# Attention and expert layers on one core: expert outputs stored from ScalarE with rings of three, small norm operations on GpSimd, second sequence of a pair in another order

## The chip, the core and the metric

The kernel runs on one core of a Trainium2 chip. The metric is the time of one execution in microseconds. A core has five engines that run side by side, each with its own queue of instructions taken strictly in order: TensorE (PE, matmul and transposes), VectorE (DVE), ScalarE (ACT), GpSimd (POOL) and SyncE (SP, which here only issues DMAs). They are held together by semaphores, and by nothing else: the order in each queue is written out by hand.

## The reference, cut to what matters

128 sequences of 128 tokens, 256 channels. First a layer of windowed attention over another input, then a layer of 16 experts of which each token takes two, each behind a layer norm and a gate.

```python
x = x + tanh(g_xattn) * xattn(layernorm(x), ctx, ctx, wq, wk, wv, wo_w, wo_b)
x = x + tanh(g_ffn)  * ffn(layernorm(x), w_router, w_fc, w_gate, w_proj)

# xattn: q, k with rotary tables, 16 heads of 16, softmax over |key - query| <= 64, projection
scores = einsum('bhnqd,bhnkd->bhnqk', qb, kband) * sqrt(dk)
out = einsum('bhnqk,bhnkd->bhnqd', softmax(where(valid, scores, neg)), vband)

# ffn: per sequence, the 2 best of 16 experts; the first 16 tokens of an expert's list are kept
top_k_probs, positions, indices, expert_inputs = vmap(dispatch)(x, softmax(x @ w_router))
h = silu(expert_inputs @ w_gate) * (expert_inputs @ w_fc)
y = vmap(collect)(h @ w_proj, indices, positions, top_k_probs)   # sum of 2 weighted rows
```

## The kernel before

Every product is made in float32 by splitting each operand into a rounded head and a rest (`..._hi`, `..._lo`) and adding three matmuls (`split_matmul`). So next to the matmuls there are many copies (heads, on ScalarE) and subtractions (rests, on VectorE and GpSimd).

**Attention (`attention_block`, L90 to L853).** The 128 sequences go in 64 pairs. One `step(s)` on each engine works on several pairs at once: scores, softmax and values of pair s, projections of s + 1, norm and context of s + 2, statistics of s + 3, output projection of s - 1, second norm and router of s - 2. Within a pair sequence 0 comes first, then sequence 1. For each sequence: `scores` (TensorE) fills four PSUM banks ST; `partial_max` (VectorE, L496) takes their maxima; `turn_max` transposes them; `shift_of` (VectorE, L503 and L507) makes the shift; `subtract_max` (TensorE) adds it to ST; `exp_unit` (ScalarE, L352, four of them) makes the probabilities; `values_unit` (TensorE, L705) multiplies them with the values. ST is one set of banks, so the scores of the next sequence wait for the last exponential. PO, one bank, holds the turned maxima and then the values.

The orders that matter here, of one step:

- ScalarE: out_t of (s-1, 1), `normed` (L427), `normed2` (L435), `attention_head` (L393), four exponentials of sequence 0, out_t, x2t, `key_head` (L398), `copy_values` (L387), `copy_logits_t` (L381), `query_heads` (q_head L405 and the two masked copies L410), `context_head` (L370), `query_rests` (L418), four exponentials of sequence 1, `input_head` (L364).
- VectorE, second half: `partial_max(s, 1)`, `norm_stats(s+3)` (L543 to L553), `keep_logits` (L587), `shift_of(s, 1)`, `normalise(s, 0)` (L515, L517), `residual(s-1)` (L566), `residual_stats` (L573 to L583), `input_rest` (L524).
- GpSimd: `scale_of_norm2` (L319 and L321), `scale_of_norm` (L278 and L280), `residual` (L271), `rotate` of k and q (L295, L296), `query_rest` (L312), `key_rest` (L303), `context_rest` (L284).

A layer norm is spread over three engines: VectorE makes mean and variance, then `nm` = -mean and `ve` = variance + eps (128x2 elements each); GpSimd makes `rstd` = ve^-0.5 and `off` = nm * rstd; ScalarE applies them.

**Routing (L856 to L993)** makes the table of places between the two; the change doesn't touch it.

**Experts (`expert_block`, L1030 to L1302).** 128 units, one per step; a unit is a sequence where tokens are moved, and two of the 16 experts of a group of eight sequences where products are made. `step(u)` does each stage for unit u - lag, with the lags LOAD -13, PICK -11, DISPATCH -9, GATE 0, HIDDEN 2, OUTPUT 3, FETCH 12, COLLECT 14. So in step u VectorE collects unit u - 14, whose rows GpSimd fetched in step u - 12. Buffers are rings: `eo`, `first`, `second`, `y_sb` have two slots, `x_in_sb` and `xr` four. GpSimd and SyncE have the steps written out flat (`run_flat`); ScalarE, VectorE and TensorE loop over 16 of them (`run`). The places that matter:

- SyncE, per step: wait for `out_done` of this step's collect, store `out` (L1118); load `xn2` (L1124); wait for `eo_copied`, store `eo_d`, 256 KB (L1129); load `xr`, 128 KB (L1134).
- GpSimd, per step: wait for the group's `eo_out` and for `out_done` of the unit two before (the ring of `first` and `second`), two indirect gathers (L1150), then `x_lo` (L1159).
- VectorE, per step: `h_lo` (L1205), `pick` (L1210), `y_part` (L1220), `gated` (L1228), `hid` (L1232), `y_sb` (L1237), `s_lo` (L1243).
- ScalarE, per step: `eo` (L1171, waits for the store of two units before), `h_hi` (L1176), `x_hi` (L1182), `th` (L1187), `s_hi` (L1193).

## Time and profile before

| | |
|---|---|
| median of 3 runs | 1889.34 us (1888.83 to 1892.42) |
| the profiled execution | 1888.86 us, span of its instructions 1887.1 us |
| mean granted TensorE clock | 0.957 |
| attention, routing, experts | 0 to about 1240, 1240 to 1340, 1340 to 1887 us |
| busy in attention (480 to 864 us) | PE 89%, DVE 82%, ACT 73%, POOL 51% |
| busy in experts (1429.5 to 1805 us) | PE 83%, DVE 83%, POOL 72%, ACT 52%, DMA 75% |

Times are microseconds from the start of the span. "PE" is TensorE's matmuls, "PEld" its weight loads, SPq the issues on SyncE's queue. A busy engine isn't necessarily the one that sets the pace: in both stages no engine is over 90%, so the waits between engines have to be read.

### The profile page before, as it was taken

The numbers are of one execution on the slowest core, as the hardware profiler recorded it, in microseconds if no ns is written. First come the engines' busy times: TensorE is split into PE (matmuls) and PEld (weight loads), VectorE is DVE, ScalarE is ACT, GpSimd is POOL, SyncE is SP. The second block draws the span as 40 slices with busy tenths as digits, with TensorE's granted clock in tenths as the row PEclk, the third lists the DMA queues.
The fourth block names the chain that finished last, engine by engine and source line by source line (L and its number), as shares of the span: only waits on it lengthen the run. The fifth ranks groups of instructions, "written<-read, shape, count | busy, mean of one in ns | idle before, by whom it ended". The sixth has DMA issues, their size and how long they took to land. (4 is left out here: it accounts for less than half of the span.)

```text
span 1887.1 us, 51499 instructions
## 1 busy us (share of the span) xinstructions
PE 1528.9 (81%) x16844; PEld 1200.2 (64%) x16844; DVE 1483.6 (79%) x3249; ACT 1165.1 (62%) x2321; POOL 1023.6 (54%) x1234
## 2 busy tenths in 40 slices
PE   4888888888888888888888888961597888788870
PEld 3566666666666666666666666640487777777760
DVE  3788888888888888888888888859788888888863
ACT  3777677777777776777777777742364555555530
POOL 3545555545545454555555545427346677677755
PEclk9999999999999999999999999975699999999995
DMA  2121212122121212121212122420257777777775
GB/s 87 46 84 56 83 56 76 63 71 68 65 74 57 82 56 83 56 83 56 83 56 81 58 68 71 137 89 12 62 170 224 231 240 236 229 240 236 239 212 178
DMA packets 156085, 210.12 MB, mean 111 GB/s; under 512 B 18688, under 2 KB 104832, under 8 KB 156032
## 3 DMA queue, kind: packets, MB, share of 16 engines
q1 hardware_dynamic: 143744, 175.92, 28.8%
q0 software_dynamic: 12288, 33.57, 6.4%
q8 instruction: 24, 0.39, 0.1%
q14 instruction: 29, 0.24, 0.0%
HBM read 125.54 MB, written 83.89 MB: 111 GB/s over the span
## 5 line engine op out<-in xcount | busy, mean ns | idle before, releaser
L496 DVE TRANSPOSE_TENSOR_REDUCE part_max<-ST 128x16 f32<-128x512 f32 x512 | 321.1, 684 | 151.0 <-PE ST L678 151.0
L705 PE MATMUL PO<-probs_t,v_aug 128*32 128x128 f32 x4096 | 206.1, 285 | 79.1 <-ACT probs_t L352 59.2
L352 ACT ACTIVATE probs_t<-ST 128x512 f32<-128x512 f32 x512 | 264.3, 602 | 8.6 <-PE ST L693 8.6
L705 PEld LDWEIGHTS PO<-probs_t,v_aug 128*32 128x32 f32 x4096 | 84.9, 108 | 194.8 <-ACT probs_t L352 188.2
L312 POOL TENSOR_TENSOR q_rest<-q_rot,q_head 128x512 f32<-128x512 f32 x64 | 82.5, 1289 | 217.3 <-ACT q_head L405 217.3
L295 POOL TENSOR_TENSOR k_rot<-k_cos,k_sin 128x256 f32<-128x256 f32 x64 | 47.2, 737 | 259.0 <-DVE k_sin L534 259.0
L1171 ACT ACTIVATE eo<-EO 128x512 f32<-128x512 f32 x128 | 76.6, 598 | 177.6 <-DMA eo_d<-eo 177.1
L1150 POOL DMA_INDIRECT first<-eo_d,collect_row x128 | 123.3, 963 | 107.1 <-DVE y_sb L1237 84.3
L1253 PE MATMUL GU<-we_hi,s_hi 128*128 128x256 f32 x512 | 156.2, 305 | 0.1
L1150 POOL DMA_INDIRECT second<-eo_d,collect_row x128 | 125.4, 980 | 42.8 <-issue 36.3
L1254 PE MATMUL GU<-we_hi,s_lo 128*128 128x256 f32 x512 | 145.5, 284 | 0.0
L1255 PE MATMUL GU<-we_lo,s_hi 128*128 128x256 f32 x512 | 144.9, 283 | 0.0
L1159 POOL TENSOR_TENSOR x_lo<-scaled,x_hi 128x256 fp32r<-128x256 f32 x128 | 109.1, 853 | 49.9 <-ACT x_hi L1182 47.6
L1253 PE MATMUL EO<-we_hi,h_hi 128*128 128x256 f32 x256 | 80.8, 316 | 54.9 <-ACT h_hi L1176 34.8
L1182 ACT ACTIVATE x_hi<-scaled 128x256 fp32r<-128x256 f32 x128 | 53.4, 417 | 113.4 <-PE DS L1298 67.7
L393 ACT ACTIVATE at_hi<-F 128x512 fp32r<-128x512 f32 x64 | 38.3, 598 | 133.1 <-PE F L723 133.1
L1297 PE MATMUL DS<-pick,x_hi 128*128 128x256 f32 x256 | 78.0, 325 | 51.4 <-DVE s_lo L1243 24.5
L1220 DVE SCALAR_TENSOR_TENSOR y_part<-first,weight,scaled 128x256 f32<-128x256 f32 x128 | 69.1, 540 | 58.2 <-DMA second<-eo_d,collect_row 54.6
L319 POOL TENSOR_TENSOR rstd<-ve,mhalf 128x2 f32<-128x2 f32 x64 | 44.9, 702 | 124.1 <-DVE ve L583 124.1
L358 ACT ACTIVATE out_t<-PO 128x512 f32<-128x512 f32 x128 | 76.7, 599 | 56.6 <-PE PO L705 53.2
L427 ACT ACTIVATE xn<-x_in_sb,off,rstd 128x256 f32<-128x256 f32 x128 | 70.0, 594 | 64.1 <-POOL off L280 64.1
L723 PE MATMUL F<-ident_sb,xn 128*128 128x128 f32 x512 | 85.7, 291 | 28.6 <-ACT xn L427 19.3
(158 smaller groups left out, 5731.0 us busy)
## 6 DMA issues: line engine op xcount, KB each, us to landing
eo_d<-eo SPq DMA_DIRECT2D x128, 256.0 KB, 2.6
x_in_sb<-x SPq DMA_DIRECT2D x64, 256.0 KB, 2.8
c_in_sb<-ctx_t SPq DMA_DIRECT2D x64, 256.0 KB, 2.8
xr_sb<-x SPq DMA_DIRECT2D x64, 256.0 KB, 4.0
x_d<-x SPq DMA_DIRECT2D x64, 256.0 KB, 4.0
xn_d<-xn SPq DMA_DIRECT2D x64, 256.0 KB, 4.2
scaled<-xn_d SPq DMA_DIRECT2D x128, 128.0 KB
scaled<-x_d SPq DMA_DIRECT2D x128, 128.0 KB
```

Of the source, the lines that this page charges most:

```text
L312: pool.tensor_tensor(q_rest[:].rearrange("p k t -> p (k t)"), q_rot[:].rearrange("p k t -> p (k t)"), q_head[:].rearrange("p k t -> p (k t ...
L352: act.activation(probs_t[:, b, i].rearrange("p j q -> p (j q)"), ST[i][:], ACT.Exp) \
L358: act.activation(out_t[:, b].rearrange("p i q -> p (i q)"), PO[:], ACT.Copy).then_inc(M["ot_copied"], 1)
L496: dve.tensor_reduce(part_max[:, i, 0], ST[i][:].rearrange("p (c l) -> p c l", l=32), AX_X, ALU.max, apply_transpose=True).then_inc(M["part ...
L705: last = pe.matmul(PO[32 * j:32 * j + 32, i * SEQ:(i + 1) * SEQ], v_aug[:, n.par, b, head], probs_t[:, b, i, j], start=True, stop=True)
L723: last = pe.transpose(F[:, (2 * k + b) * SEQ:(2 * k + b + 1) * SEQ], src[:, b, k * P:(k + 1) * P], ident[:])
L1150: pool.indirect_dma_start(out=dst[:, n.slot(2)], out_offset=None, in_=D["eo_d"][n.group].rearrange("r e c -> (r e) c"), in_offset=bass.Ind ...
L1159: pool.tensor_tensor(x_lo[:, n.slot(2)], x_in_sb[:, n.slot(4)], x_hi[:, n.slot(2)].bitcast(F32), ALU.subtract).then_inc(M["x_lo_done"], 1)
L1253: pe.matmul(out, lh, rh, start=first, stop=False)
L1254: pe.matmul(out, ll, rh, start=False, stop=False)
L1255: return pe.matmul(out, lh, rl, start=False, stop=last)
L1297: pe.matmul(out, x_hi[:, n.slot(2), k * P:(k + 1) * P], pick[:, n.slot(2)], start=True, stop=False)
```

## The change

Four things, all in the order or the place of work; what is computed stays.

1. Norms: `nm` and `ve` (and `nm2`, `ve2`) are made on GpSimd, right before `rstd`, instead of on VectorE after the aggregates. GpSimd waits for `ln_aggr` instead of `ve_done`.
2. Attention, sequence 1 of a pair. VectorE: `shift_of(s, 1)` before `keep_logits`, `residual` before `normalise`. TensorE: `logits_t` after `output_projection(.., 1)`, `subtract_max` before `untranspose`, `inputs_t` between `values_unit` 1 and 2. ScalarE: q_head and the masked copies before `copy_values`, `context_head` after the exponentials.
3. Experts: the store of `eo_d` is issued by ScalarE, behind `h_hi`. `eo`, `first`, `second`, `x_in_sb`, `xr` are rings of three. So the store is waited for three units later, and a gather waits for the collect of three units before, which is the step before its own. `y_part` is written in place in `y_sb` (its wait for the store of `out` moves up by one instruction), `gated` in place in `th`.
4. Experts: ScalarE and VectorE are written out flat too.

```diff
         def scale_of_norm(n):
+            pool.wait_ge(M["ln_aggr"], (n + 1).n)
+            wait_for(pool, M["xn_done"], n.n)
+            pool.sem_inc(M["pool_passed"], 1)
+            pool.tensor_scalar(ve[:], mv[:, :, 1], EPS, None, ALU.add).then_inc(M["ve_done"], 1)
+            pool.tensor_scalar(nm[:], mv[:, :, 0], -1.0, None, ALU.mult)
             pool.wait_ge(M["ve_done"], (n + 1).n)
-            wait_for(pool, M["xn_done"], n.n)
             pool.tensor_tensor(rstd[:], ve[:], mhalf[:], ALU.pow).then_inc(M["rstd_done"], 1)
...
             if (s + 1).real:
                 key_head(s + 1)
+                query_head(s + 1)
+                masked_heads(s + 1)
                 copy_values(s + 1)
             if (s - 2).real:
                 copy_logits_t(s - 2)
             if (s + 1).real:
-                query_heads(s + 1)
-            if (s + 2).real:
-                context_head(s + 2)
-            if (s + 1).real:
-                query_rests(s + 1)
+                masked_rests(s + 1)
             if s.real:
                 for i in range(4):
                     exp_unit(s, 1, i)
             if (s + 2).real:
+                context_head(s + 2)
                 input_head(s + 2)
...
-            dve.wait_ge(M["ln_aggr"], (n + 1).n)
-            wait_for(dve, M["off_done"], n.n)
-            dve.tensor_scalar(nm[:], mv[:, :, 0], -1.0, None, ALU.mult)
-            dve.tensor_scalar_add(ve[:], mv[:, :, 1], EPS).then_inc(M["ve_done"], 1)
...
                 norm_stats(s + 3)
+            if s.real:
+                shift_of(s, 1)
             if (s - 2).real:
                 keep_logits(s - 2)
+            if (s - 1).real:
+                residual(s - 1)
             if s.real:
-                shift_of(s, 1)
                 normalise(s, 0)
             if (s - 1).real:
-                residual(s - 1)
                 residual_stats(s - 1)
...
                 output_projection(s - 1, 0)
-            if (s - 2).real:
-                logits_t(s - 2)
             if s.real:
                 turn_max(s, 1)
             if (s - 1).real:
                 output_projection(s - 1, 1)
+            if (s - 2).real:
+                logits_t(s - 2)
             if s.real:
+                subtract_max(s, 1)
                 untranspose(s, 0)
-                subtract_max(s, 1)
+                values_unit(s, 1, 0)
+                values_unit(s, 1, 1)
             if (s + 2).real:
                 inputs_t(s + 2)
             if s.real:
-                for i in range(4):
-                    values_unit(s, 1, i)
+                values_unit(s, 1, 2)
+                values_unit(s, 1, 3)
...
-            n = unit(OUTPUT)
-            if on(OUTPUT):
-                sp.wait_ge(M["eo_copied"], n.n + 1)
-                sp.dma_start(D["eo_d"][n.group][:, n.j * 2:n.j * 2 + 2], eo[:, n.slot(2)]) \
-                    .then_inc(eo_out[n.slot(2)], 16)
             n = unit(FETCH)
             if on(FETCH):
-                wait_for(sp, M["y_part_done"], n.n - 3)
...
+                wait_for(sp, M["y_part_done"], n.n - 2)
...
-                wait_for(pool, M["out_done"], n.n - 1)
+                wait_for(pool, M["out_done"], n.n - 2)
...
                 act.wait_ge(M["eo_done"], n.n + 1)
-                wait_for(act, eo_out[n.slot(2)], (n - 2).landed(2))
-                act.activation(flat(eo[:, n.slot(2)]), EO[n.slot(2)][:], ACT.Copy).then_inc(M["eo_copied"], 1)
+                wait_for(act, eo_out[n.turn(3)], (n - 3).landed(3))
+                act.activation(flat(eo[:, n.turn(3)]), EO[n.slot(2)][:], ACT.Copy).then_inc(M["eo_copied"], 1)
...
+            n = unit(OUTPUT)
+            if on(OUTPUT):
+                act.wait_ge(M["eo_copied"], n.n + 1)
+                act.dma_start(D["eo_d"][n.group][:, n.j * 2:n.j * 2 + 2], eo[:, n.turn(3)]) \
+                    .then_inc(eo_out[n.turn(3)], 16)
...
-                dve.wait_ge(rows_in[n.slot(2)], n.landed(2, 32))
-                dve.wait_ge(x1_in[n.slot(4)], n.landed(4))
-                wait_for(dve, M["out_done"], n.n)
-                dve.scalar_tensor_tensor(out=y_part[:], in0=first[:, n.slot(2)],
+                dve.wait_ge(rows_in[n.turn(3)], n.landed(3, 32))
+                dve.wait_ge(x1_in[n.turn(3)], n.landed(3))
+                wait_for(dve, y_out[n.slot(2)], (n - 2).landed(2))
+                dve.scalar_tensor_tensor(out=y_sb[:, n.slot(2)], in0=first[:, n.turn(3)],
...
-        run(dve, step)
+        run_flat(dve, step)
```

## Rows read from the trace of the kernel before

**Rows 1.** First and last start of an instruction of each step: attention, early experts, collects, tail.

```profile
L364 ACT ACTIVATE xt_hi<-F x57: 628/628/628, 110.9 to 1182.0; 128x512 fp32r<-128x512 f32 x57
L1193 ACT ACTIVATE s_hi<-DS x10: 589/591/593, 1359.4 to 1385.6; 128x512 fp32r<-128x512 f32 x10
L1237 DVE SCALAR_TENSOR_TENSOR y_sb<-second,weight,y_part x96: 476/686/1072, 1429.7 to 1801.0; 128x256 f32<-128x256 f32 x96
L1237 DVE SCALAR_TENSOR_TENSOR y_sb<-second,weight,y_part x15: 479/485/485, 1838.4 to 1884.4; 128x256 f32<-128x256 f32 x15
```

**Rows 2.** Timeline (start, duration, what, [idle before]), sequence 1 of a pair in attention.

```profile
603.30 1.29 POOL L312 TENSOR_TENSOR q_rest<-q_rot,q_head 128x512 f32<-128x512 f32 x1 [3.44 <-ACT q_head L405]
603.42 0.33 PE L686 MATMUL PO<-ident_sb,part_max 128*128 128x128 f32 x1
603.54 1.07 DVE L552 TENSOR_SCALAR nm<-mv 128x2 f32<-128x2 f32 x1
604.70 0.28 DVE L503 TENSOR_REDUCE PO<-PO 128x32 f32<-128x128 f32 x1
605.01 0.69 DVE L507 TENSOR_TENSOR shift<-PO,own_sb 128x512 fp32r<-128x512 f32 x1
605.08 1.32 ACT L418 ACTIVATE q_lo<-q_rest,qmask_sb 128x512 fp32r<-128x512 f32 x2
606.38 2.06 ACT L352 ACTIVATE probs_t<-ST 128x512 f32<-128x512 f32 x4
608.21 0.17 DVE L582 TENSOR_SCALAR nm<-mv 128x2 f32<-128x2 f32 x1
```

**Rows 3.** Timeline, from there to the next pair's first exponentials.

```profile
605.77 1.29 POOL L284 TENSOR_TENSOR ct_lo<-c_in_sb,ct_hi 128x512 fp32r<-128x512 f32 x1
608.31 0.63 ACT L364 ACTIVATE xt_hi<-F 128x512 fp32r<-128x512 f32 x1
608.61 0.70 POOL L319 TENSOR_TENSOR rstd<-ve,mhalf 128x2 f32<-128x2 f32 x1 [1.55 <-DVE ve L583]
609.39 0.20 POOL L321 TENSOR_TENSOR off<-nm,rstd 128x2 f32<-128x2 f32 x1
610.63 1.10 ACT L427 ACTIVATE xn<-x_in_sb,off,rstd 128x256 f32<-128x256 f32 x2 [1.04 <-POOL off L280]
614.84 0.60 ACT L393 ACTIVATE at_hi<-F 128x512 fp32r<-128x512 f32 x1 [2.13 <-PE F L723]
615.41 2.07 ACT L352 ACTIVATE probs_t<-ST 128x512 f32<-128x512 f32 x4
...
627.66 0.63 ACT L364 ACTIVATE xt_hi<-F 128x512 fp32r<-128x512 f32 x1
```

**Rows 4.** The chain (start, duration, what) through two steps of the expert stage.

```profile
1636.62 0.49 DVE y_sb L1237
...
1639.15 3.59 DMA second<-eo_d,collect_row
...
1644.65 0.48 DVE y_sb L1237
```

**Rows 5.** The chain, elsewhere in the same stage: the load of xr.

```profile
1605.21 4.24 DMA scaled<-x_d
```

**Rows 6.** Groups, 1429.5 to 1805 us: count | busy us, mean ns | idle before.

```profile
L1159 POOL TENSOR_TENSOR x_lo<-scaled,x_hi 128x256 fp32r<-128x256 f32 x96 | 84.4, 879 | 2.0
L1171 ACT ACTIVATE eo<-EO 128x512 f32<-128x512 f32 x96 | 57.4, 598 | 138.0 <-DMA eo_d<-eo 137.9
```

**Rows 7.** Timeline of the expert stage, GpSimd and VectorE.

```profile
1601.24 0.42 DVE L1205 TENSOR_TENSOR h_lo<-HT,h_hi 128x256 fp32r<-128x256 f32 x1 [0.47 <-ACT h_hi L1176]
...
1604.39 0.42 DVE L1205 TENSOR_TENSOR h_lo<-HT,h_hi 128x256 fp32r<-128x256 f32 x1
...
1604.59 0.96 POOL L1150 DMA_INDIRECT first<-eo_d,collect_row  x1 [0.19 <-issue]
...
1606.83 0.75 POOL L1159 TENSOR_TENSOR x_lo<-scaled,x_hi 128x256 fp32r<-128x256 f32 x1
```

More of the change, by code:

```diff
@@ L1025, in slot, with turn @@
         return self.c % ring
+    def turn(self, ring):
+        return self.n % ring
     def landed(self, ring, each=16):
-        return (self.i * (LOOP // ring) + self.c // ring + 1) * each
+        return (self.n // ring + 1) * each
 def expert_block(nc, ctx, T, D):
@@ L1055, in expert_block @@
     th = sb("th", [P, 2, 2, HID])
-    gated = sb("gated", [P, 2, HID])
     hid = sb("hid", [P, 2, 2, HID])
@@ L1059, in expert_block @@
     h_lo = sb("h_lo", [P, 2, 2, P], F32R)
[L1060 to L1064 removed]
+    eo = sb("eo", [P, 3, 2, DIM])
+    first = sb("first", [P, 3, DIM])
+    second = sb("second", [P, 3, DIM])
     ident, iota = T["ident2"], T["iota"]
@@ L1158, in step @@
                 wait_for(pool, M["ds_done"], n.n - 1)
-                pool.tensor_tensor(x_lo[:, n.slot(2)], x_in_sb[:, n.slot(4)], x_hi[:, n.slot(2)].bitcast(F32),
+                pool.tensor_tensor(x_lo[:, n.slot(2)], x_in_sb[:, n.turn(3)], x_hi[:, n.slot(2)].bitcast(F32),
                                    ALU.subtract).then_inc(M["x_lo_done"], 1)
@@ L1235, in step @@
                 dve.wait_ge(M["y_part_done"], n.n + 1)
-                wait_for(dve, y_out[n.slot(2)], (n - 2).landed(2))
-                dve.scalar_tensor_tensor(out=y_sb[:, n.slot(2)], in0=second[:, n.slot(2)],
-                                         scalar=weight[:, 1, bass.ds(n.n, 1)], in1=y_part[:],
+                dve.scalar_tensor_tensor(out=y_sb[:, n.slot(2)], in0=second[:, n.turn(3)],
+                                         scalar=weight[:, 1, bass.ds(n.n, 1)], in1=y_sb[:, n.slot(2)],
                                          op0=ALU.mult, op1=ALU.add).then_inc(M["out_done"], 1)
```

72 lines of the change are left out of this document (35 added, 37 removed).

## The prediction

> **What bounds the kernel now.** I read the pace of each stage first. In attention a pair takes (1182.0 - 110.9) / 56 = 19.13 us [rows 1]. In the expert stage a step takes (1801.0 - 1429.7) / 95 = 3.91 us while products are made, and (1884.4 - 1838.4) / 14 = 3.29 us in the tail, where only rows are collected; the first steps, before anything is collected, took (1385.6 - 1359.4) / 9 = 2.91 us [rows 1]. So TensorE could do a step in 2.9 us, and collecting costs a microsecond more.
>
> Then what closes the circle in each stage. *Experts:* the chain of waits runs from one collect to the collect two steps later [rows 4]. `y_sb` ends at 1637.11; the first gather and the issue of the second take it to 1639.15, and the second one's landing 3.59 us more; `y_sb` of that unit ends at 1645.13. That is 8.02 us for two steps, 4.01 per step, against 3.91 measured. The circle has two steps because the ring of `first` and `second` has two slots. A second circle of the same length runs over SyncE: `y_sb`, store of `out`, load, store of `eo_d`, load of `xr`, which landed 4.24 us after its issue began [rows 5], with three issues of nearly half a microsecond ahead of it. ScalarE sat idle for 138.0 us before 96 `eo` copies, 1.44 us each, for a store of `eo_d` to land [rows 6]. *Attention:* no engine is full, the work goes through all of them in turn. Between turned maxima (ready at 603.75) and VectorE's `neg` (604.70) nearly a microsecond is lost: VectorE is held in `nm`, 1.07 us for two elements per partition, which ends with GpSimd's `q_rest` (603.30 + 1.29 = 604.59); the same instruction took 0.17 us at 608.21 with GpSimd idle [rows 2]. ScalarE is late as well: `q_lo` ends at 606.40 and the exponentials start at 606.38, though the shift was ready at 605.70.
>
> **The change, part by part.** *Sequence 1 in attention.* `nm` leaves VectorE and `shift_of` goes ahead of `keep_logits`, so `neg` waits for the turned maxima alone: 604.70 becomes about 603.7, as `logits_t` no longer stands ahead of `turn_max` either. The shift is ready 1.0 us earlier, at about 604.7. ScalarE must be free by then. It moves q_head and the masked copies into the time that it waited for the value projection, and `context_head` (0.6 us) behind the exponentials; `q_rest` starts earlier and ends before `q_lo` wants it. I get ScalarE free at about 604.5. So the exponentials start 1.0 us earlier. `inputs_t`, now between values 1 and 2, fills a gap in which TensorE waits for exponentials; `untranspose` runs beside the first one. Gain 1.0 us per pair up to the end of the exponentials, bounds 0.6 and 1.1.
>
> *What is late next.* From that end E (608.44 in [rows 2]) to the next pair's first exponential took 615.41 - 608.44 = 6.97 us [rows 3]. This pair is one of the longer: 627.66 - 608.31 = 19.35 [rows 3] against the mean of 19.13 [rows 1], so the mean is 6.75 and the shorter ones, which alternate with these, have about 6.5. The moves put a new chain here. `context_head` 0.5, then `ct_lo` on GpSimd 1.29, which used to be done long before E (605.77 to 607.06) and now stands in front of the norms. Then per norm two added operations, `rstd` 0.70, 0.08 of wait, `off` 0.20. Then `xn` and, as long, `xn2` on ScalarE, 1.0 each, and `at_hi` 0.6, ahead of the exponentials in ScalarE's order [rows 3]. The price of an added GpSimd operation on 128x2 is in no row. The nearest are `off`, 0.20 (a plain multiply of the same size), and `rstd`, 0.70 (a power) [rows 3]; VectorE's own 0.17 [rows 2] bounds it from below. I take 0.18, a plain multiply with its overlap. Sum: 0.5 + 0.1 + 1.25 + 2 x (0.36 + 0.94) + 0.1 + 2.0 + 0.6 = 7.15 us. That is 0.4 more than the mean 6.75. It was covered before by the 1.04 and 2.13 us that ScalarE idled for `off` and for the transposed attention [rows 3]; both covers are used up. So the net is 1.0 - 0.4 = 0.6 to 0.65 per pair; over some 60 pairs 39 us. By the ends of the price: at 0.17 nothing changes, at 0.70 the sum is 2.1 us longer, and a pair loses 1.5 us instead. The other readers in that stretch have room: key projection wants `ct_lo`, ready at E + 1.9, only behind the next scores and a transpose, and VectorE's `xt_lo`, which may end a little after those scores, is covered by ScalarE's chain.
>
> The rows show VectorE's `nm` held until GpSimd's instruction is over [rows 2]. [...]
>
> *Rings of three.* The gather now waits for the collect of the step before its own. The circle of 8.0 us has three steps in place of two: 2.7 per step, no longer a bound. In the tail the circle is shorter (3.29 x 2 = 6.6), so 2.2 per step, about GpSimd's own two gathers: 2.24 from first to `x_lo` [rows 7]. I take 2.35.
>
> *The store of `eo_d` on ScalarE.* SyncE loses one issue of about 0.5 us and 256 KB ahead of `xr` in its queue. The `xr` circle, 1.4 + 4.24 + 2.1 from `y_part` to the end of `y_sb` = 7.7 per two steps, becomes 0.9 + 3.0 to 4.24 + 2.1, 3.0 to 3.6 per step; without those 256 KB I place it at the lower end, under the next bound. With three slots `eo` has a step more to land, and the 1.44 us of ScalarE go. ScalarE pays the issue, about 0.5 us beside 52% of 3.91, 2.0 of work: 2.5 per step. Queued behind it are `x_hi`, `th`, `s_hi`; VectorE waits for `th`. That is under the next bound too. The price on ScalarE is in no row; between nothing and 1 us I take SyncE's 0.5. `x_in_sb` and `xr` lose a slot; SyncE then waits for `x_lo` and `y_part` of the step before, both done before the `out_done` for which it waits anyway: nothing.
>
> *What is late next in the expert stage.* GpSimd: first gather at 1604.59, `x_lo` at 1606.83 for 0.75 to 1.0 us (mean 0.88), 0.19 of issue [rows 6, 7]: 2.24 + 0.88 + 0.19 = 3.3 us. VectorE: from `h_lo` at 1601.24 to `h_lo` at 1604.39 without a wait but one: 3.15 us, with a `y_sb` of 0.55; with the median `y_sb` of 0.69 it is 3.3 [rows 1, 7]. Written flat, it also drops some register operations. Two engines at 3.3 that hold each other up: I take 3.45, bounds 3.3 and 3.75. Steps with collect and products: about 113, 113 x (3.91 - 3.45) = 51 us. Tail: 14 x (3.29 - 2.35) = 13 us. Experts 64 us.
>
> **Sum.** The profiled execution took 1888.86 us (span 1887.1 and 1.8 around it), 0.5 under the median of the runs shown. 1889 - 39 - 64 = 1786 us.
>
> **The rivals.** *Experts gain, attention doesn't.* An added GpSimd operation costs about 0.35, or ScalarE isn't free when the shift is ready: the chain behind E takes back the whole microsecond. 1889 - 64 = 1825. For it: the chain was worked out to 7.15 against 6.5 in half of the pairs, so there is little room. Against: a plain multiply was 0.20. Chance 0.22.
>
> *VectorE's collects wait for GpSimd.* [...] GpSimd, now 72% busy, would be over 90%, and if each `y_sb` took its longest, 1.07, and `y_part` as much more, a step would be 3.15 + 0.5 + 0.3 = 3.9: only the tail and attention gain, 1889 - 39 - 13 = 1837. For it: the spread of `y_sb` and `x_lo` in [rows 1, 7]. [...] Halfway, at 3.7, it is 1815. [...] Chance 0.15 for 1815 to 1840.
>
> *Better than forecast.* Attention keeps the whole microsecond (60 us) and a step falls to 3.3 (69 us): 1889 - 60 - 69 - 13 = 1747. Chance 0.12 for under 1765.
>
> *Slower.* The four added operations stand in series on GpSimd between E and the next exponentials. At x us each they cost 60 x 4 x (x - 0.18) more than in the sum, against 103 us gained: the sum turns at x = 0.18 + 103 / 240 = 0.61. At 0.70, the price of `rstd`, it is 1786 + 125 = 1911. For it: a GpSimd operation is long for its size. Against: the 0.20 of `off`. Chance 0.03.
>
> *It doesn't do what it says:* the gathers still wait for `out_done`, since GpSimd waits for `eo_out` of the whole group, which lands later. The last store of a group is issued two steps before its first gather, and a landing as long as that of [rows 5] fits in 6.9. Then a group would lose up to 1 us, 16 in all: 1802, inside the forecast.
>
> **How the numbers follow.** Forecast 1786 with a range of its own from 1765 to 1812, chance 0.48. The range for 8 in 10 takes in the attention rival and half of the lock rival, and part of the better case: 1752 to 1836. A measurement of this kernel can tell 0.2% from no change, 1885.6 to 1893.1. Faster 0.95, within 0.02, slower 0.03.
>
> **What would show it.** Attention right: `neg` follows the turned maxima at once, the exponentials start about 0.6 us behind the shift and ScalarE has no idle time between `xn` and `at_hi`; a pair takes 18.5 us. Wrong: GpSimd's added operations are over 0.3 us, or `q_lo` still ends with the start of the exponentials. Experts right: no idle time before `eo` for a store, gathers not behind `y_sb`, 3.45 us a step and 2.35 in the tail. Wrong: `y_sb` and `y_part` near a microsecond, or idle time before `y_part` for `xr`. The prediction fails most if either engine finds a new partner to wait for that I haven't costed.

## The result, and the profile after

The changed kernel took 1835.47 us (median of 4 runs, 1834.73 to 1839.67), the kernel before 1889.93 beside it: ratio 0.9717, with an interval of 0.9696 to 0.9737. The forecast was 1786. The direction was right, and the gain was about half of what the sum said. The time lies outside the range that the forecast gave itself, 1765 to 1812, and half a microsecond inside the range for 8 in 10, 1752 to 1836. The profiled execution took 1835.99 us, with a span of 1834.2.

| stretch | before | after | forecast |
|---|---|---|---|
| start to the first `y_sb` (attention, routing, first expert steps) | 1398.1 us | 1402.5 us | -39 us |
| a pair in attention | 19.13 us | 19.20 us | 18.5 us |
| collects 0 to 113 | 440.3 us | 393.1 us | -51 us |
| an expert step | 3.91 us | 3.46 us | 3.45 us |
| the 14 steps of the tail | 45.9 us | 36.0 us | -13 us |
| mean granted TensorE clock | 0.957 | 0.936 | |

An expert step is the mean from collect 0 to collect 103, here and below; up to collect 113 the mean is 3.90 before and 3.48 after.

So the experts gave 57 us where 64 were expected, and attention gave back 4 where 39 were expected. The rows that answer to [rows 1] are these: first `xt_hi`, one per pair, then `y_sb` while products are made and in the tail. `y_sb` now goes by the name `scaled`, since the rings share one tile; its input `second` tells it from `y_part`.

```profile
L372 ACT ACTIVATE xt_hi<-F x57: 617/620/622, 112.0 to 1187.2; 128x512 fp32r<-128x512 f32 x57
...
L1243 DVE SCALAR_TENSOR_TENSOR scaled<-second,weight,scaled x105: 477/701/1066, 1402.5 to 1761.4; 128x256 f32<-128x256 f32 x105
L1243 DVE SCALAR_TENSOR_TENSOR scaled<-second,weight,scaled x15: 478/485/551, 1795.6 to 1831.5; 128x256 f32<-128x256 f32 x15
```

**Attention: sequence 1 went as forecast.** The rows below (start, duration, what, idle before) answer to [rows 2]. The turned maxima are no longer held behind `nm`: the reduction is followed by the shift and, 0.67 us behind the shift's end (607.72 + 0.69 = 608.41), by the exponentials.

```profile
606.64 1.33 ACT L428 ACTIVATE q_lo<-q_rest,qmask_sb 128x512 fp32r<-128x512 f32 x2
607.41 0.28 DVE L512 TENSOR_REDUCE PO<-PO 128x32 f32<-128x128 f32 x1
607.72 0.69 DVE L516 TENSOR_TENSOR shift<-PO,own_sb 128x512 fp32r<-128x512 f32 x1
609.08 2.07 ACT L360 ACTIVATE probs_t<-ST 128x512 f32<-128x512 f32 x4 [1.12 <-PE ST L699]
```

The first line and the last show something that the forecast missed: ScalarE is done at 607.97 and then idles 1.12 us before the exponentials. That is the place in which `context_head`, 0.65 us, used to stand. This pair is one of the long ones (see below); in the pair before it the idle time is 0.83 us, still more than `context_head` takes.

**Attention: what is late next.** The stretch that answers to [rows 3], one pair earlier:

```profile
589.03 2.06 ACT L360 ACTIVATE probs_t<-ST 128x512 f32<-128x512 f32 x4 [0.83 <-PE ST L699]
590.96 0.65 ACT L378 ACTIVATE ct_hi<-c_in_sb 128x512 fp32r<-128x512 f32 x1
591.68 1.29 POOL L288 TENSOR_TENSOR ct_lo<-c_in_sb,ct_hi 128x512 fp32r<-128x512 f32 x1 [4.16 <-ACT ct_hi L378]
593.06 0.22 POOL L324 TENSOR_SCALAR ve<-mv 128x2 f32<-128x2 f32 x1
593.36 0.22 POOL L325 TENSOR_SCALAR nm<-mv 128x2 f32<-128x2 f32 x1
593.54 0.71 POOL L327 TENSOR_TENSOR rstd<-ve,mhalf 128x2 f32<-128x2 f32 x1
595.88 0.20 POOL L284 TENSOR_TENSOR off<-nm,rstd 128x2 f32<-128x2 f32 x1
596.11 1.09 ACT L437 ACTIVATE xn<-x_in_sb,off,rstd 128x256 f32<-128x256 f32 x2 [3.53 <-POOL off L284]
598.09 0.58 ACT L401 ACTIVATE at_hi<-F 128x512 fp32r<-128x512 f32 x1
598.57 2.04 ACT L360 ACTIVATE probs_t<-ST 128x512 f32<-128x512 f32 x4
599.20 1.14 PE L711 MATMUL PO<-probs_t,v_aug 128*32 128x128 f32 x16 [1.53 <-ACT probs_t L360]
```

This is the chain that the prediction named, read from the top: GpSimd waits 4.16 us for `ct_hi`, makes `ct_lo`, then both norms (593.06 to 596.08), and ScalarE waits 3.53 us for `off` with nothing else to do; behind it stand `xn`, `xn2`, `at_hi` and only then the exponentials. From the end of the exponentials, 591.09, to the next ones, 598.57, it is 7.48 us where 7.15 were forecast; the mean over all pairs is 7.52, and 6.73 before the change. The last row is what was not forecast: TensorE idles 1.53 us before the values of sequence 0.

**What TensorE's clock does then.** Pairs now have two lengths, 18.66 and 20.1 us, and about 3 of 8 are long. Two windows of 3 us, one in a long pair and one in the short pair after it, show why (columns: window, PE busy, PEld, DVE, ACT, POOL, granted clock, DMA share, GB/s):

```profile
600.00:603.00 3.00, 3.00 (x40) 1.99 (x36) 0.59 (x1) 1.06 (x3) 1.41 (x2) 0.50 0.84 264
...
620.00:623.00 3.00, 3.00 (x61) 2.12 (x54) 1.14 (x3) 2.19 (x5) 1.69 (x3) 1.00 0.83 305
```

Right after the idle 1.53 us the granted clock is 0.50, and TensorE does 40 matmuls in 3 us; in the next pair the clock is 1.00, and it does 61 in the same time. Between 100 and 1190 us there are 22 such stretches, 75 us in all; before the change there was none. In the pairs from 119 us on, each of them begins 0.4 to 1.5 us behind the idle time before the values of sequence 0, which is 1.30 to 1.55 us long in every pair; before the change it was 0.77. Whole attention, before and after:

```profile
110.00:1190.00 1080.00, 962.88 (x12152) 710.34 (x12149) 886.90 (x2035) 784.06 (x1469) 550.52 (x735) 1.00 0.22 70
```
```profile
110.00:1190.00 1080.00, 965.28 (x12119) 731.02 (x12119) 825.39 (x1802) 755.26 (x1463) 600.28 (x956) 0.97 0.21 68
```

TensorE is as busy as before for the same work, although the wait behind it is longer. That the slow stretches and the missing gain are one thing is for the experiments.

**Experts.** Groups of 1400 to 1770 us (count | busy us, mean ns | idle before, and for what), answering to [rows 6]:

```profile
L1174 ACT ACTIVATE eo<-EO 128x512 f32<-128x512 f32 x106 | 63.6, 600 | 12.3 <-issue 5.0 <-PE EO L1261 3.8 <-remote 2.3
L1190 ACT ACTIVATE x_hi<-scaled 128x256 fp32r<-128x256 f32 x103 | 43.0, 418 | 145.8 <-DMA scaled<-xn_d 87.9 <-PE DS L1304 57.0 <-issue 0.9
L1162 POOL TENSOR_TENSOR x_lo<-scaled,x_hi 128x256 fp32r<-128x256 f32 x104 | 96.8, 931 | 2.1
L1243 DVE SCALAR_TENSOR_TENSOR scaled<-second,weight,scaled 128x256 f32<-128x256 f32 x106 | 76.2, 719 | 0.0
L1153 POOL DMA_INDIRECT first<-eo_d,collect_row x107 | 105.1, 982 | 32.1 <-issue 18.3 <-DVE scaled L1243 12.0 <-DMA eo_d<-eo 1.5
```

The 138 us for which ScalarE waited for a store are gone, and a gather hardly waits for `y_sb`, 12.0 us over 107 steps. In place of both ScalarE waits 87.9 us, before `x_hi`, for the load of `xn2` to land. One turn of that circle (SPq and ACTq are the issues on the two queues):

```profile
1504.25 1.06 DVE L1243 SCALAR_TENSOR_TENSOR scaled<-second,weight,scaled 128x256 f32<-128x256 f32 x1
...
1504.54 0.33 ACTq L1184 DMA_DIRECT2D eo_d<-eo  x1
...
1505.34 0.34 SPq L1126 DMA_DIRECT2D out<-scaled  x1
1505.78 0.45 SPq L1132 DMA_DIRECT2D scaled<-xn_d  x1
...
1509.88 0.42 ACT L1190 ACTIVATE x_hi<-scaled 128x256 fp32r<-128x256 f32 x1 [1.67 <-DMA scaled<-xn_d]
...
1511.40 0.75 DVE L1243 SCALAR_TENSOR_TENSOR scaled<-second,weight,scaled 128x256 f32<-128x256 f32 x1
```

`y_sb` ends, the store of `out` goes out, then the load of `xn2`; when it has landed, `x_hi` runs, and behind `x_hi` in their queues the work that leads to the `y_sb` two steps later: 1512.15 - 1505.31 = 6.84 us for two steps. Over the stage the parts are 0.48 from the end of `y_sb` to the issue, 3.65 to the landing, 0.40 to `x_hi`, 2.37 to the end of `y_sb`: 6.90 per two steps, 3.45 per step. The load landed in about 2.5 us before the change and in about 3.65 after it; `xr`, whose landing was expected to be quicker, went from about 3.8 to 3.6. (These times run from an issue to the last landing event that the trace holds of the transfer. In some runs not all of these events were recorded, so they are good to 0.1 us at best.)

### The profile page after: what moved, and what is told of

The parts are those of the page before. It is cut to its first block and busy times, and to the rows that moved or that the text cites. A ratio compares the mean times of both kernels' runs of the same rounds, so it can differ in the third digit from the quotient of the medians.

```text
span 1834.2 us, 50716 instructions
## 1 busy us (share of the span) xinstructions
PE 1520.0 (83%) x16843; PEld 1222.3 (67%) x16844; DVE 1410.9 (77%) x2993; ACT 1133.7 (62%) x2321; POOL 1088.1 (59%) x1490
## 5 line engine op out<-in xcount | busy, mean ns | idle before, releaser
L288 POOL TENSOR_TENSOR ct_lo<-c_in_sb,ct_hi 128x512 fp32r<-128x512 f32 x64 | 82.4, 1288 | 278.0 <-ACT ct_hi L378 278.0
L711 PEld LDWEIGHTS PO<-probs_t,v_aug 128*32 128x32 f32 x4096 | 94.4, 114 | 204.5 <-ACT probs_t L360 192.6
L1162 POOL TENSOR_TENSOR x_lo<-scaled,x_hi 128x256 fp32r<-128x256 f32 x128 | 115.2, 900 | 48.8 <-ACT x_hi L1190 46.7
L729 PE MATMUL F<-ident_sb,xn 128*128 128x128 f32 x512 | 91.8, 306 | 31.6 <-ACT xn L437 19.7
L679 PE MATMUL ST<-q_hi,k_hi 32*128 32x256 f32 x1024 | 94.6, 358 | 5.9 <-issue 5.4
L1260 PEld LDWEIGHTS GU<-we_hi,s_lo 128*128 128x128 f32 x512 | 98.6, 192 | 0.0
L1261 PEld LDWEIGHTS GU<-we_lo,s_hi 128*128 128x128 f32 x512 | 98.1, 192 | 0.0
L1259 PEld LDWEIGHTS GU<-we_hi,s_hi 128*128 128x128 f32 x512 | 97.9, 191 | 0.2 <-issue 0.2
L1259 PEld LDWEIGHTS EO<-we_hi,h_hi 128*128 128x128 f32 x256 | 49.0, 191 | 72.9 <-issue 63.2
```

Of the source, the lines that this page charges most:

```text
L288: pool.tensor_tensor(ct_lo[:].rearrange("p k b t -> p (k b t)"), c_in_sb[:, n.par].rearrange("p k b t -> p (k b t)"), ct_hi[:].rearrange(" ...
L679: pe.matmul(ST[i][:, m * 2 * SEQ:(m + 1) * 2 * SEQ], k_part[rows, n.par, m, b], q_part[rows, n.par, m, b].rearrange("p e t -> p (e t)"), s ...
L711: last = pe.matmul(PO[32 * j:32 * j + 32, i * SEQ:(i + 1) * SEQ], v_aug[:, n.par, b, head], probs_t[:, b, i, j], start=True, stop=True)
L729: last = pe.transpose(F[:, (2 * k + b) * SEQ:(2 * k + b + 1) * SEQ], src[:, b, k * P:(k + 1) * P], ident[:])
L1162: pool.tensor_tensor(x_lo[:, n.slot(2)], x_in_sb[:, n.turn(3)], x_hi[:, n.slot(2)].bitcast(F32), ALU.subtract).then_inc(M["x_lo_done"], 1)
L1259: pe.matmul(out, lh, rh, start=first, stop=False)
```

## The experiments

Ratios are against the kernel before on the same chip; its median moved from 1889.9 to 1896.4 us between groups of runs, so ratios are compared and not times. "Slow" is the number of stretches at a granted clock of 0.50 between 100 and 1190 us.

| run | us | ratio | pair | slow | step | tail step |
|---|---|---|---|---|---|---|
| before | 1889.9 | 1 | 19.13 | 0 | 3.91 | 3.28 |
| after | 1835.5 | 0.9717 | 19.20 | 22 | 3.46 | 2.57 |
| e1 context early | 1760.9 | 0.9315 | 17.97 | 1 | 3.46 | 2.50 |
| e2 filler | 1800.6 | 0.9515 | 18.65 | 0 | 3.47 | 2.55 |
| e3 norms only | 1899.3 | 1.0035 | 19.20 | 7 | 3.91 | 3.33 |
| e4 order only | 1838.3 | 0.9713 | 18.25 | 1 | 3.96 | 3.32 |
| e5 experts only | 1836.3 | 0.9697 | 19.12 | 0 | 3.52 | 2.53 |
| e6 two slots | 1885.5 | 0.9934 | 19.23 | 23 | 3.79 | 3.18 |
| e7 store on SyncE | 1868.1 | 0.9866 | 19.23 | 23 | 3.73 | 2.65 |
| e8 short `x_lo` | 1872.6 | 0.9888 | 19.25 | 25 | 3.77 | 2.44 |
| e9 load first | 1823.4 | 0.9607 | 19.22 | 23 | 3.36 | 2.54 |
| e10 e1, loads first | 1744.7 | 0.9188 | 17.96 | 1 | 3.38 | 2.50 |
| e11 e1, norms on VectorE | 1783.2 | 0.9403 | 18.29 | 1 | 3.53 | 2.48 |
| e12 flat only | 1896.6 | 0.9994 | 19.12 | 0 | 3.96 | 3.33 |
| e13 e9 with short `x_lo` | 1869.7 | 0.9862 | 19.19 | 21 | 3.78 | 2.58 |

**e1: `context_head` back where it stood, in the changed kernel.**

```diff
+            if (s + 2).real:
+                context_head(s + 2)
             if (s + 1).real:
                 masked_rests(s + 1)
...
             if (s + 2).real:
-                context_head(s + 2)
                 input_head(s + 2)
```

> The changed kernel with one move undone: ScalarE's context_head stands ahead of the masked rests again, not behind the exponentials. [...] A pair takes 18.0 us in place of 19.2: about 1765 us. Rival B (the added GpSimd operations alone are the bound): the exponentials come hardly earlier, 18.6 us per pair without the slow stretches, 1800 us. [...]

The 18.0 us expected took the next exponentials as 0.6 to 0.7 us earlier, TensorE's idle time before the values of sequence 0 as 0.8 us in place of 1.5, and its clock as kept; with the new order of sequence 1 as the cause of the slow stretches it would have been 1825 to 1835 us.

Measured: ratio 0.9315 (0.9294 to 0.9336), 75 us less than the changed kernel; a pair takes 17.97 us in the mean and no pair over 18.2.

```profile
590.03 1.28 POOL L288 TENSOR_TENSOR ct_lo<-c_in_sb,ct_hi 128x512 fp32r<-128x512 f32 x1
591.45 2.06 ACT L360 ACTIVATE probs_t<-ST 128x512 f32<-128x512 f32 x4 [0.26 <-PE ST L700]
597.04 1.09 ACT L437 ACTIVATE xn<-x_in_sb,off,rstd 128x256 f32<-128x256 f32 x2 [2.21 <-POOL off L284]
599.64 0.60 ACT L401 ACTIVATE at_hi<-F 128x512 fp32r<-128x512 f32 x1 [0.52 <-PE F L730]
600.84 0.92 PE L712 MATMUL PO<-probs_t,v_aug 128*32 128x128 f32 x16 [0.77 <-ACT probs_t L360]
```

In this timeline `ct_lo` ends before the exponentials of sequence 1 even start, ScalarE idles 0.26 us before them in place of 1.12, and 2.21 before `xn` in place of 3.53. TensorE idles 0.77 us before the values in place of 1.53, and the one slow stretch that is left begins at 1174 us, when the last pairs run out. One move of one 0.65-us copy costs the changed kernel 1.2 us per pair. It holds both causes, though, the shorter chain and the kept clock; e2 takes them apart.

**e2: the late chain stays, but TensorE has something to do during the idle time.** Eight transposes of the identity, into a part of PO that nobody reads at that time, between `subtract_max(s, 0)` and the values.

```diff
                 subtract_max(s, 0)
+                for _ in range(8):
+                    pe.transpose(PO[:, 3 * P:4 * P], ident[:], ident[:])
```

> The changed kernel with eight transposes of the identity added on TensorE, between subtract_max and the values of sequence 0, into a part of PO that the values overwrite; nothing is left out. They take 1.1 us where TensorE idles 1.5 us. [...] Rival (the clock falls with work, or TensorE's own time is the bound): stretches stay, and the added work costs up to 1.1 us per pair: 1835 to 1900 us.

If the clock falls because TensorE idles there, 18.6 to 18.7 us per pair and about 1802 us were expected.

Measured: 0.9515 (0.9497 to 0.9533), every pair 18.65 us (18.58 to 18.73), no slow stretch. The filler computes nothing and saves 35 us, and the chain is as long as in the changed kernel, 7.52 us in the mean. So it gives the clock's share alone. Attention of e1, then of e2, answers to the two rows of before and after:

```profile
110.00:1190.00 1080.00, 994.45 (x12840) 754.59 (x12836) 868.82 (x1905) 818.66 (x1547) 631.30 (x1007) 1.00 0.24 77
```
```profile
110.00:1190.00 1080.00, 1020.51 (x12919) 781.73 (x12921) 847.79 (x1849) 775.37 (x1506) 619.27 (x986) 1.00 0.22 73
```

The granted clock is 1.00 in both. Each of the 22 stretches had lengthened a pair by 20.1 - 18.66 = 1.45 us, 32 us in all, near the 35 that came back. What remains from e2 to e1, 18.65 to 17.97, is 0.68 us per pair, some 40 us, for the chain itself.

**e3 and e4: the first part alone, and the second part alone, in the kernel before.**

```diff
+            pool.tensor_scalar(ve[:], mv[:, :, 1], EPS, None, ALU.add).then_inc(M["ve_done"], 1)
+            pool.tensor_scalar(nm[:], mv[:, :, 0], -1.0, None, ALU.mult)
...
-            dve.tensor_scalar(nm[:], mv[:, :, 0], -1.0, None, ALU.mult)
-            dve.tensor_scalar_add(ve[:], mv[:, :, 1], EPS).then_inc(M["ve_done"], 1)
```

> The kernel before with part 1 of the change alone: nm and ve on GpSimd, nothing reordered, experts as before. VectorE's stall of 0.9 us in nm goes, but the exponentials of sequence 1 waited for ScalarE's q_lo as well, so they start when they did. GpSimd's off comes 1.1 us later; ScalarE's idle time of 2.1 us before at_hi covers that. Theory A: 19.1 us per pair, 1887 to 1892 us. Rival B (the added operations are what took the gain back): 19.5 or more per pair, 1910 us.

```diff
             if s.real:
+                shift_of(s, 1)
+            if (s - 2).real:
+                keep_logits(s - 2)
...
             if (s + 2).real:
+                context_head(s + 2)
                 input_head(s + 2)
```

> The kernel before with part 2 of the change alone: the new order of sequence 1, with nm and ve left on VectorE. q_rest is over before nm starts, so there is no stall, and the shift is about as early as in the changed kernel. The chain behind the exponentials is 1.1 us shorter than in the changed kernel, as the four added operations are missing. Theory A: at full clock 18.0 to 18.3 us per pair and few or no slow stretches: 1830 to 1845 us with experts as before. Rival B (context_head behind the exponentials isn't the matter, the shift is late again without part 1): 19.0 or more, 1885 us.

Measured: e3 1.0035 (1.0021 to 1.005), with 7 slow stretches; e4 0.9713 (0.9684 to 0.9741), a pair 18.25 us, with one. The new order alone, with the norms still on VectorE, is worth all that the whole change is worth, 0.88 us per pair. Moved by itself, the norms' work is a small loss, and that too is the clock's: the trace of e3 has 7 long pairs of 20.74 us, as many as slow stretches, while the others take 18.98 in the mean, under the 19.13 of before. TensorE's longest idle time before values is shorter there than in the changed kernel; this row stands just ahead of a slow stretch that begins at 495.7 us.

```profile
493.24 1.88 PE L708 MATMUL PO<-probs_t,v_aug 128*32 128x128 f32 x32 [0.97 <-ACT probs_t L360]
```

In e3 such idle times come twice in a pair, 0.97 and 0.77 us, where the kernel before has 0.77 once and no slow stretch. So the two parts are not a sum: e4 without the four added operations in the late chain keeps its clock, and the changed kernel, with both, loses it.

**e11: e1 without the first part.** `nm` and `ve` as in e3's removed lines, the rest as e1.

> e1 with part 1 of the change undone: nm and ve on VectorE again, ahead of shift_of. It shows what the move to GpSimd is worth once the order is right. [...] Rival B (the stall in nm comes back in full, against k_lo): 1 us per pair, 1820 us.

If the move to GpSimd is worth only the stall in `nm`, a pair within 0.3 us of e1's and 1750 to 1778 us were expected.

Measured: 0.9403 (0.9387 to 0.9418), a pair 18.29 us, against 17.97 in e1.

```profile
599.71 0.17 DVE L554 TENSOR_SCALAR nm<-mv 128x2 f32<-128x2 f32 x1
```

`nm` takes 0.17 us here, on VectorE, where [rows 2] had 1.07. Before the change it started 0.95 to 1.05 us ahead of the end of GpSimd's `q_rest` (480 to 860 us); in the new order it starts 0.02 to 0.13 us ahead of the end of `k_lo`. The norms on GpSimd are still worth 0.3 us per pair, which is not the stall that they were counted for. It fits the two instructions that stood ahead of the shift: from the first exponentials of a pair to the last it takes 11.44 us in e11 and 11.16 in e1, and the chain behind them is the same, 6.8. With `context_head` early they gain, with it late (e4 18.25, after 18.65 at full clock) they lose: it is the place of `ct_lo` that decides.

**e5: third and fourth part alone. e12: only ScalarE and VectorE written out flat.**

```diff
-        run(act, step)
+        run_flat(act, step)
...
-        run(dve, step)
+        run_flat(dve, step)
```

> The kernel before with the expert parts of the change alone (rings of three, the store of eo_d on ScalarE, ScalarE and VectorE written flat); attention as before. If the parts add up, the expert stage gives the 57 us that it gave in the changed kernel (3.45 us per step, 2.55 in the tail), and attention, which is as before, 0: 1833 us, within 3 us of the changed kernel's own 1835. Rival (attention gave part of the gain, the expert stage less): 1845 or more.

> The kernel before with ScalarE and VectorE of the expert stage written flat, nothing else. The two-step circle over the gathers stays the bound; what goes are register operations of 0.06 us, of which about three stand between y_part and y_sb in that circle. Theory A: 0.05 to 0.1 us per step, 1880 to 1885 us. [...]

Measured: e5 0.9697 (0.9673 to 0.9721) with 3.52 us per step and 2.53 in the tail; e12 0.9994 (0.9978 to 1.0009). The expert parts alone give as much as the whole change, and writing the loops out gives none of it.

**e6: the rings of `first` and `second` with two slots, in the changed kernel.**

```diff
-                wait_for(pool, M["out_done"], n.n - 2)
+                wait_for(pool, M["out_done"], n.n - 1)
...
-                        out=dst[:, n.turn(3)], out_offset=None,
+                        out=dst[:, n.slot(2)], out_offset=None,
```

> The changed kernel with first and second as rings of two again (the gather waits for the collect of its own step); the store of eo_d, the other rings and the flat loops stay. Theory A (the circle of collect, gather and landing had two steps and was the bound): 7.6 to 8.0 us per two steps again, 3.85 us per step and 3.3 in the tail, so 40 to 50 us of the expert gain are lost: 1880 us. Rival B (the store of eo_d was the bound): less than 10 us lost, 1845 us.

Measured: 0.9934 (0.9909 to 0.9958), 3.79 us per step and 3.18 in the tail; 37.7 and 8.6 us are lost again. The gather circle of [rows 4] was the bound, and without the third slot most of the experts' gain is gone.

**e7: the store of `eo_d` back on SyncE, between the loads, in the changed kernel.**

```diff
+                sp.wait_ge(M["eo_copied"], n.n + 1)
+                sp.dma_start(D["eo_d"][n.group][:, n.j * 2:n.j * 2 + 2], eo[:, n.turn(3)]) \
+                    .then_inc(eo_out[n.turn(3)], 16)
             n = unit(FETCH)
...
-                act.wait_ge(M["eo_copied"], n.n + 1)
-                act.dma_start(D["eo_d"][n.group][:, n.j * 2:n.j * 2 + 2], eo[:, n.turn(3)]) \
-                    .then_inc(eo_out[n.turn(3)], 16)
```

> The changed kernel with the store of eo_d back on SyncE between the load of xn2 and the load of xr; rings of three and flat loops stay. Theory A (with rings of three the circle over SyncE is 3.0 to 3.9 us per step): xr lands late again, 3.6 us per step, 15 to 20 us lost: 1853 us. Rival B (the place of the store is worth nothing once the rings are longer): 1833 to 1838 us.

Measured: 0.9866 (0.9844 to 0.9888), 3.73 us per step: 25.6 us of the collects are lost. VectorE idles 48.5 us before `y_part` between 1410 and 1750 us, where it idles 17.3 in the changed kernel; the gathered rows had landed 3 us and more before nearly all of those starts, so it is `xr` that is late, as the prediction's second circle has it. GpSimd's gathers also wait 23.7 us for a store of `eo_d` to land, against 0.2. So both circles of the prediction had to be opened; either alone leaves about 3.75.

These two runs also say something of the load of `xn2`, for which `x_hi` waits 85.8 us in the changed kernel between 1410 and 1750 us. The same stretch of e6, then of e7:

```profile
L1190 ACT ACTIVATE x_hi<-scaled 128x256 fp32r<-128x256 f32 x90 | 37.6, 418 | 158.2 <-PE DS L1304 115.0 <-issue 39.8 <-DMA scaled<-xn_d 3.4
```
```profile
L1190 ACT ACTIVATE x_hi<-scaled 128x256 fp32r<-128x256 f32 x91 | 37.9, 417 | 123.0 <-PE DS L1304 108.5 <-DMA scaled<-xn_d 14.5
```

With the store on ScalarE and two slots the load hardly keeps `x_hi` waiting, and it lands in about 2.7 us in both runs. So neither the store's move nor the rings make it late by themselves; it takes 3.2 to 3.9 us in all runs that have both and 2.2 to 2.7 in all others.

**e9: SyncE issues the load of `xn2` ahead of the store of `out`.** The store is what waits for the step's own collect. With the load ahead of it, the load waits in its queue for the collect of the step before, and the circle over the load has three steps in place of two.

```diff
-            n = unit(COLLECT)
-            if on(COLLECT):
-                sp.wait_ge(M["out_done"], n.n + 1)
-                sp.dma_start(D["out"][bass.ds(n.n, 1)].rearrange("b t c -> t b c"),
-                             y_sb[:, n.slot(2):n.slot(2) + 1]).then_inc(y_out[n.slot(2)], 16)
...
+            n = unit(COLLECT)
+            if on(COLLECT):
+                sp.wait_ge(M["out_done"], n.n + 1)
+                sp.dma_start(D["out"][bass.ds(n.n, 1)].rearrange("b t c -> t b c"),
+                             y_sb[:, n.slot(2):n.slot(2) + 1]).then_inc(y_out[n.slot(2)], 16)
             n = unit(FETCH)
```

> The changed kernel with SyncE's load of xn2 ahead of the store of out in every step of the expert stage, so that it no longer waits for this step's collect. Theory A (the new bound of a step is a circle over that load: 0.48 us from the end of y_sb to its issue, 3.65 to land, 0.40, 2.37 from x_hi to the end of y_sb, 6.90 us for two steps, where 3.45 is measured): the circle is cut, x_hi no longer waits for the load, a step takes 3.2 to 3.3 us, as in the even stretch of the changed kernel with steps of 3.2, and the kernel 1810 to 1820 us. Rival B (VectorE and GpSimd hold each other at 3.45, the load is late by coincidence): 1833 to 1838 us.  Rival C (the transfers crowd each other and land later still): 1835 or more.

Measured: 0.9607 (0.9568 to 0.9645), 3.36 us per step, 17 us less in the collects. The load now goes out before the `y_sb` of its step has even begun, on average 1.9 us before it ends, where it used to be 0.48 behind:

```profile
1503.54 0.33 SPq L1127 DMA_DIRECT2D scaled<-xn_d  x1
...
1504.85 0.50 DVE L1243 SCALAR_TENSOR_TENSOR scaled<-second,weight,scaled 128x256 f32<-128x256 f32 x1
...
1505.38 0.34 SPq L1132 DMA_DIRECT2D out<-scaled  x1
```

The group of `x_hi`, and the whole stretch:

```profile
L1190 ACT ACTIVATE x_hi<-scaled 128x256 fp32r<-128x256 f32 x104 | 43.4, 417 | 131.0 <-PE DS L1304 131.0
...
1400.00:1750.00 350.00, 319.63 (x2505) 302.47 (x2504) 337.31 (x729) 210.38 (x522) 293.98 (x313) 1.00 0.87 273
```

The wait for the load before `x_hi` is gone from its group: it was the bound after the change. What ScalarE waits for now is `DS`, and VectorE is busy for 337.3 of 350 us, 96%. So of the two engines that the prediction named as the next bound, VectorE is nearly full only here, at 3.36 us. That it sets this pace together with GpSimd (84%) is not shown: TensorE is busy for 91% and the DMA engines for 87%, and e13, which was to test it, did not.

**e8: `x_lo` over 32 of 256 columns, from the third unit on.** Left out is most of the rests of the experts' inputs; all else stays. **e13** is the same in e9.

```diff
+                cols = DIM if n.n < 2 else 32
-                pool.tensor_tensor(x_lo[:, n.slot(2)], x_in_sb[:, n.turn(3)], x_hi[:, n.slot(2)].bitcast(F32),
-                                   ALU.subtract).then_inc(M["x_lo_done"], 1)
+                pool.tensor_tensor(x_lo[:, n.slot(2), 0:cols], x_in_sb[:, n.turn(3), 0:cols],
+                                   x_hi[:, n.slot(2), 0:cols].bitcast(F32), ALU.subtract).then_inc(M["x_lo_done"], 1)
```

> The changed kernel with GpSimd's x_lo of the expert stage cut to 32 of its 256 columns from the third unit on, so the rest of the dispatched tokens is left out in part and the output is not that of the reference. It takes some 0.7 us per step off GpSimd (from 3.3 to 2.6). Theory A (GpSimd and VectorE set the 3.45 us of a step together, and VectorE's collects wait for GpSimd's reads): y_sb falls from a mean of 0.72 to 0.55 us, a step to 3.2, the kernel to 1805 us. Rival B (VectorE's own work alone): 3.4 us, 1830 us. Rival C (the load of xn2 with its ring of three, for which ScalarE's x_hi waited 86 us): x_lo ends earlier and so the load starts earlier too, the waits before x_hi go and a step falls under 3.15 us.

> e9 (load of xn2 ahead of the store of out) with GpSimd's x_lo cut to 32 of 256 columns from the third unit on, as in e8; part of the dispatched tokens is left out. With the circle over the load cut, VectorE is busy 96% of the expert stage, y_part 0.59 and y_sb 0.69 us where they take 0.48 alone. Theory A (VectorE with its waits for GpSimd is the next bound, and e8 was slow because its steps still hung on the load): y_sb and y_part at 0.48 to 0.52, a step 3.0 to 3.15 us against 3.36, ratio 0.945. Rival B (a shorter x_lo upsets the order on TensorE and ScalarE by itself, whatever the load does): 3.6 us or more per step, ratio 0.98, and what slowed e8 isn't the load.

Measured: 0.9888 (0.9868 to 0.9908) and 0.9862 (0.9826 to 0.9898). Both are slower than their partners with the whole `x_lo`, by 33 and 47 us from the first collect to collect 113, though a GpSimd instruction of 0.93 us became one of 0.32 (e8), and one of 0.90 became one of 0.31 (e13 against e9).

```profile
L1244 DVE SCALAR_TENSOR_TENSOR scaled<-second,weight,scaled 128x256 f32<-128x256 f32 x91 | 46.9, 515 | 0.0
...
L1229 DVE SCALAR_TENSOR_TENSOR scaled<-first,weight,scaled 128x256 f32<-128x256 f32 x91 | 43.7, 480 | 4.6 <-issue 3.9 <-DMA scaled<-x_d 0.7
L1191 ACT ACTIVATE x_hi<-scaled 128x256 fp32r<-128x256 f32 x93 | 38.8, 417 | 139.5 <-remote 55.2 <-PE DS L1305 53.9 <-issue 23.4
```

These rows of e8 show half of what was asked: with the GpSimd instruction short, the collects of VectorE take 0.51 and 0.48 us, where `y_sb` takes 0.72 in the changed kernel. So the whole `x_lo` does lengthen `y_sb`, by 0.2 us in the mean. But the steps don't become shorter. They fall into a rhythm of one of 2.8 us and one of 4.3 to 5.1. e13 shows the same although its load lands 5 us before `x_hi` starts in the median, so the load is not the reason. Two things come with the rhythm, in waits of e13:

```profile
POOL first L1153 <- DVE scaled L1244: 71.2, 38, 1.9
...
POOL first L1153 <- issue: 26.7, 51, 2.2
```

A gather waits again for `y_sb`, and now and then up to 2.2 us for nothing that the profile shows; in the changed kernel such a wait was 0.5 at most. The rhythm also comes with a lower clock of TensorE, 0.94 between 1400 and 1750 us in e13 against 1.00 in e9; whether that is a cause or a result of the longer waits isn't shown. What starts the rhythm is open.

**e10: e1, with both loads of SyncE ahead of its store of `out`.** The edits are those of e1 and e9, the store standing one load further down.

> Both repairs: context_head ahead of the masked rests, as in e1, and both loads of the expert stage (xn2 and xr) ahead of the store of out. If they add up and theory A on the load holds: 1761 - 20 = 1735 to 1745 us. If VectorE and GpSimd are the bound of a step: 1761, as e1.

Measured: 1744.70 us (1739.83 to 1745.25), ratio 0.9188 (0.9172 to 0.9203). This version beats both kernels: about 5% less than the changed kernel, with the same instructions in another order.

## Why the prediction was right or wrong

**What bounds the kernel before: right.** e6 gives back 3.79 us per step and 3.18 in the tail with nothing but the ring depth, and e7 shows the second circle, over SyncE, by 25.6 us and by VectorE's wait for `xr`.

**Sequence 1, "gain 1.0 us": right, and somewhat small.** From the first exponentials of a pair to the last it took 12.4 us before (19.13 - 6.75), and 11.13 in pairs at full clock after, so 1.25 less. The maxima, shift and exponentials stand as forecast. But the reason given for `nm` on GpSimd was only half right: e4 and e11 show the stall gone by the order alone (`nm` at 0.17 us in every pair).

**"What is late next", 7.15 us: right in its chain, short by 0.33.** The pair shown has 7.48. The added operations took 0.22 each where 0.18 was taken, and both norms together 3.02 us where 2.6 was taken, since there are gaps between them. At full clock a pair is 18.65 (e2), against 18.5 forecast: these terms account for 9 us of the miss.

**The step that failed is "so the net is 0.6 to 0.65 per pair", as it stopped at ScalarE.** The sum asked how much later the exponentials start and not what TensorE does meanwhile. TensorE idles 1.30 to 1.55 us before the values, its clock, 1.00 in attention before, falls to 0.50 in 22 stretches, and 32 us go, so that attention took 4 us more where 39 less were forecast. e2 shows it by taking only idle time away: 0.33 to 0.53 us are left, no stretch is slow, and 35 us come back. Over the whole of attention TensorE is as busy after the change (965 us) as before (963), so its mean share would not have told of the clock. The prediction had no term for it. With this the rival "experts gain, attention doesn't" came out, 1825 against 1835, but by another mechanism than it had named: an added operation cost 0.22, not 0.35, and ScalarE was free in time.

**"`context_head` behind the exponentials" was costed at 0.5 in the chain, and its cover was not looked for.** The prediction made room for the exponentials by moving it, though ScalarE would have had some 0.8 us to spare. e1 shows its price: 1.2 us per pair, 0.7 by the chain and the rest by the clock.

**Experts, 3.45 us per step: the number was right by luck, the bound was not.** GpSimd and VectorE "at 3.3 that hold each other up" were said to be next. Next was the circle over the load of `xn2`, 6.90 us per two steps, which is in none of the prediction's sums. With the load as quick as before, 2.5 us, that circle would have given 2.9 per step; at 3.65 it gave 3.45. The prediction took it that fewer bytes ahead in SyncE's queue make loads quicker and costed `xr` so: 3.0 at the lower end. That holds in e6, where `xr` lands in 2.9, but not in the changed kernel, where it took 3.6. That landings become longer when both parts of the change are in was in no term, and why they do is open. e9 shows the bound by cutting the circle. A step then takes 3.36, so a new bound lies close behind, which of the engines it is being open.

**The store's price on ScalarE, 0.5: smaller.** The issue took 0.33, and ScalarE had idle time around it.

**Tail, 2.35: mis-sized.** It took 2.57 per step, 36.0 - 14 x 2.35 = 3 us more. The collects before it gave 47 us where 51 were forecast.

**"The collects wait for GpSimd": a real effect, not the bound.** The prediction's range calls this the lock rival, and no run shows a lock: what they show is `y_sb` at 0.72 us in the mean beside the whole `x_lo` and at 0.51 beside the short one (e8). From the kernel before to the changed one the median of `y_sb` went from 0.69 to 0.70 us in the rows like [rows 1], not to 1.07, and 3.7 to 3.9 us per step did not come. What GpSimd's `x_lo` costs the step could not be told by shortening it.

**Slower, and "it doesn't do what it says": neither.** An added operation cost 0.22 against a turning point of 0.61, and gathers waited 4.6 us in the whole stage for stores.

The sum as it should have stood: attention 60 x (18.65 - 19.13) = -29 and clock +32, experts -47, tail -10: 1889 - 54 = 1835.

## What to carry to other kernels

Where a change makes one engine's work late, ask what TensorE does in that time: an idle stretch that costs little by itself can cost the clock (here 1.30 to 1.55 us per pair, and 32 us in all by stretches at 0.50), and a filler that computes nothing tells in one run how much. Before an instruction is moved to make room, look whether the engine would have idled there in any case. When a ring gets deeper, write down each circle through a load as well as through a gather, and leave room for landing times to grow (here from 2.5 to 3.65 us), since the circle that wasn't listed can be the next bound.

## What was not expected of the hardware

- In attention TensorE's granted clock stood at 1.00 throughout with one idle time of 0.77 us per pair before the values, and fell to 0.50 in 22 stretches with one of 1.30 to 1.55 us, and in none with eight transposes in that time. The same kernel has short and long pairs, 18.66 and 20.1 us, by that alone. With two idle times per pair, 0.97 and 0.77 us (e3), it fell in 7 stretches. How much idle time it takes is therefore not told by its length alone, and stays open.
- A load of SyncE's, `xn2`, became slower, 2.5 to 3.65 us from issue to landing, when the 256-KB store behind it moved to ScalarE and the rings grew to three. The move by itself is not the reason: in e6 the store is on ScalarE too, and the load lands in 2.7. The share of time that the core's DMA engines are busy does not settle it either: 77% in e6, 78% in e8, where the load takes 3.2, and 86% in the changed kernel. The move paid all the same (e7).
- A GpSimd `tensor_scalar` on 128x2 took 0.22 us, and an issue 0.33 us on ScalarE against 0.45 on SyncE for the same store (medians, 1400 to 1750 us).
- A shorter GpSimd instruction made the expert step longer (e8, e13: 3.46 to 3.77 and 3.36 to 3.78 us). The cause is open.
